# Attention and feed-forward on one core: a guard flag computed under held-back value products, and input loads in tiles

## The reference

```python
xn = layernorm(x)
q, k, v = xn @ Wq.T, xn @ Wk.T, xn @ Wv.T          # q: 4 groups x 8 heads x 16, k and v: 8 heads x 16
probs = softmax(q k^T * 16**-0.5)                  # per batch, group and head, over 2048 keys
a_dot = probs @ v
sigma_q = elu(q.reshape(b, s, 4, 128))
a_mem = sigma_q @ memory / (sigma_q @ memory_norm)
x = x + a_dot * (1 - w) + a_mem * w                # w = sigmoid(memory_weight)
y = float8(layernorm(x) / input_scale)             # rounded to float8_e4m3, clipped at 448
out = x + (y * input_scale) @ (weight * weight_scale).T
```

## Time and profile before

| | us |
|---|---|
| median of 3 runs | 2056.89 (2056.71 to 2058.98) |
| profiled execution | 2056.68 |
| its span | 2055.0 |
| busy: PE / ACT / DVE / POOL | 2029.6 / 1934.2 / 1112.6 / 83.8 |
| first projection on the chain | 16.41 |
| chunk 7's first projection | 182.07 |
| first exponential | 211.51 |

### The profile page before, as it was taken

The page is one execution under the profiler, slowest core; times in us unless marked ns, Lnnn a source line. Parts: engine busy times, 40 slices in busy tenths (PEclk is TensorE's granted clock), DMA queues, the critical chain, the costliest instruction groups (busy, mean ns, idle before and its releaser), DMA issues.

```text
span 2055.0 us, 63328 instructions
## 1 busy us (share of the span) xinstructions
PE 2029.6 (99%) x27756; PEld 905.6 (44%) x27756; DVE 1112.6 (54%) x1721; ACT 1934.2 (94%) x2181; POOL 83.8 (4%) x141
## 2 busy tenths in 40 slices
PE   8999999999999999999999999999999999999998
PEld 4555344434444444444444444444444444444445
DVE  5776544555455554555545555455554555545555
ACT  4555899999999999999999999999999999999997
POOL 3322000000000000000000000000000000000000
PEclk9999999999999999999999999999999999999999
DMA  5656211112211211112211222111112111121111
GB/s 193 195 187 207 63 47 29 43 49 51 51 33 48 72 51 45 34 47 70 51 47 38 69 51 51 48 48 50 50 51 50 54 49 51 51 64 35 47 49 46
DMA packets 137563, 131.64 MB, mean 64 GB/s; under 512 B 31520, under 2 KB 113824, under 8 KB 137312
## 3 DMA queue, kind: packets, MB, share of 16 engines
q1 hardware_dynamic: 135248, 125.11, 22.0%
q10 hardware_dynamic: 2064, 2.69, 0.4%
HBM read 86.57 MB, written 37.49 MB: 60 GB/s over the span
## 4 chain that ended last, share of the span: by engine, by line
PE 97%; DVE 1%; ACT 0%; DMA 0%; issue 0%; ACTq 0%; POOL 0%; DVEq 0%; POOLq 0%
PE ps L763 43%; PE ps L785 42%; PE ps L708 6%; PE ps L823 1%; PE ps L809 1%; PE ps L723 1%; PE ps L677 1%; PE ps L876 1%; PE ps L893 1%; DMA mem_aug<-in_memory_norm 0%; PE ps L924 0%; DVE ps L1068 0%; DVE pool L956 0%; DVE parts L981 0%; PE ps L692 0%
## 5 line engine op out<-in xcount | busy, mean ns | idle before, releaser
L645 ACT ACTIVATE pool<-ps 128x1024 f32<-128x1024 f32 x1953 | 1795.2, 1158 | 9.6 <-PE ps L763 6.5
L763 PE MATMUL ps<-q_st,k_st 99*32 99x512 bf16 x16128 | 1103.8, 379 | 3.2 <-issue 3.2
L785 PE MATMUL ps<-pool,v_st 128*32 128x512 f32 (+1 forms) x8568 | 1063.1, 567 | 0.0
L763 PEld LDWEIGHTS ps<-q_st,k_st 99*32 99x32 bf16 x16128 | 451.5, 96 | 804.8 <-issue 490.3
L785 PEld LDWEIGHTS ps<-pool,v_st 128*32 128x32 f32 x8568 | 276.6, 110 | 202.9 <-issue 0.5
L1152 DVE STREAM_TRANSPOSE by_token<-ps 128x512 f32<-128x512 f32 x63 | 45.2, 717 | 476.7 <-PE ps L785 476.7
L1145 DVE SCALAR_TENSOR_TENSOR parts<-parts 128x1024 f32<-128x1024 f32 x189 | 231.6, 1225 | 6.5
L1131 DVE TENSOR_SCALAR parts<-ps 128x512 f32<-128x512 f32 x126 | 87.1, 691 | 131.6 <-PE ps L763 131.6
L708 PE MATMUL ps<-pool,wqT 128*128 128x512 f32 x256 | 111.4, 593 | 0.0
L600 ACT ACTIVATE parts<-ps 128x512 bf16<-128x512 f32 x40 | 23.9, 597 | 62.6 <-PE ps L708 62.6
L1208 DVE SCALAR_TENSOR_TENSOR y_out<-ps,scalars,resid 128x512 f32 (+1 forms) x28 | 21.0, 751 | 112.9 <-PE ps L809 112.9
(11 more groups left out here) (126 smaller groups left out, 836.8 us busy)
## 6 DMA issues: line engine op xcount, KB each, us to landing
q_st<-q_aug SPq DMA_DIRECT2D x384, 64.0 KB
v_st<-v_aug SPq DMA_DIRECT2D x64, 256.0 KB
q_aug<-parts SPq DMA_DIRECT2D x96, 128.0 KB
k_st<-k_aug SPq DMA_DIRECT2D x64, 192.0 KB
sigma_kept<-y_out SPq DMA_DIRECT2D x32, 256.0 KB, 3.9
k_st<-k_aug SPq DMA_DIRECT2D x64, 128.0 KB
wqT<-sigma_kept SPq DMA_DIRECT2D x32, 256.0 KB, 3.4
resid<-in_x SPq DMA_DIRECT2D x7, 1024.0 KB, 8.9
```

Of the source, the lines that this page charges most:

```text
L645: act.activation(held[:, half_u * 2 * CH:half_u * 2 * CH + 2 * CH], sc[unit % SLOTS].rearrange("p a b -> p (a b)"), ACT.Exp, scale=EXP_UNIT)\
L763: last = pe.matmul(dst[VW * c:VW * c + VW, :], k_st[0:AUG, par, keys:keys + VW], q_st[0:AUG, par, q * CH:q * CH + CH], start=True, stop=True)
L785: last = pe.matmul(acc[par][VW * c:VW * c + VW, :].rearrange("v (i s) -> v i s", s=VW)[:, places, :], v_st[:, par, j, :], by_place[:, c, p ...
```

## The change

- Loads: chunk 0 of x comes as four DMAs of one tile and Wq as four of 128 rows, the first two of Wq on ScalarE's queue, the others on SP's once x's first tile has landed; Wk, Wv and the small loads move to SP's queue behind them. Statistics of chunk 0 wait for each tile.
- Start on TensorE: 20 turns of the identity come first; Wq is turned by row blocks as they land; the last two strips of x are turned between the first projection's matmuls; Wk's and Wv's turns and copies come after that projection. ScalarE loads its table at the start, with an exponential that nothing uses. The exponential of the memory weight and the wait for the scalars come later.
- The rows of ones of the key operand come by DMA instead of a GpSimd memset.
- Key norms of chunk c move behind the first projection of chunk c + 1, their reduction behind VectorE's first rest there.
- Chunk 6 has no value product. In chunk 7 the query norms come before the last matmul pair of the key projection, then the values of chunk 6 (in bank 1) and 7, with the key norms, the mean key norm and the ranges' turns between their tiles. The squares of chunk 7's keys are taken by ScalarE from PSUM. VectorE takes the guard's sums first, the key's rest after them, and the last two third parts after the flag.
- Two units of scores are computed before TensorE reads the flag; `scores_ready` is raised for them after it.
- VectorE's late tile uses `work`, decoding and rounding use `parts`. Its waits for stores move: for the parts to the decoding, for sigma behind the first chunk's heads.
- Tail: product 2 comes before turn 3, and between them 20 turns of the identity.

The core of the diff:

```diff
+            for t in range(TPC):
+                act.dma_start(resid[:, t, :], x_tiles[:, t, :]).then_inc(x_tile_loaded[t], 16)
+            for a in range(KT // 2):
+                act.dma_start(wq_raw[:, a, :], Wq[a * P:a * P + P, :]).then_inc(wq_loaded[a], 16)
...
+            sp.wait_ge(x_tile_loaded[0], 16)
+            for a in range(KT // 2, KT):
+                sp.dma_start(wq_raw[:, a, :], Wq[a * P:a * P + P, :]).then_inc(wq_loaded[a], 16)
...
-            pool_e.memset(k_st[ROWS:P, :, :], 1.0).then_inc(ones_set, 1)
...
+            def square_keys(c):
+                act.wait_ge(proj_ready, c * (QG + 1) + QG + 1)
+                act.wait_ge(n2_ready, 2 * c)
+                act.activation(k_sq[:, :], pj[(c * (QG + 1) + QG) % len(pj)], ACT.Square).then_inc(sq_ready, 1)
...
+            for i in range(WARM_UP_TURNS):
+                pe.transpose(n2[:, 0:P], ident[:, :], ident[:, :])
...
+                    if c > 0 and o == 0:
+                        key_norms(c - 1)
...
+            def last_chunk(c, par):
+                for o in range(QG + 1):
+                    pe.wait_ge(part3_ready, c * (QG + 1) + o - len(pj) + 1)
+                    if o < QG:
+                        project(c, par, o, range(KT))
+                    if o == 0:
+                        key_norms(c - 1)
+                project(c, par, QG, range(KT - 1))
+                query_norms(c)
+                project(c, par, QG, range(KT - 1, KT))
+                project_v(c - 1, 1 - par, 0)
+                key_norms(c)
+                for t in range(1, TPC):
+                    project_v(c - 1, 1 - par, t)
+                    if t == TPC - 2:
+                        mean_key_norm(1)
+                pe.wait_ge(v_tile_ready, c - 1)
+                project_v(c, par, 0)
+                pe.wait_ge(range_ready, 2)
...
+                last.then_inc(ranges_ready, 1)
+                for t in range(1, TPC):
+                    project_v(c, par, t)
...
-            pe.wait_ge(w_copied, 2)
-            turn_xn(0, range(KT))
-            pe.wait_ge(w_copied, KT + 2)
-            pe.wait_ge(scal, 4)
...
+            turn_xn(0, range(KT // 2))
+            pe.wait_ge(w_copied, KT)
+            for k in range(KT // 2):
+                project(0, 0, 0, range(k, k + 1))
+                turn_xn(0, range(KT // 2 + k, KT // 2 + k + 1))
+            project(0, 0, 0, range(KT // 2, KT))
+            for j in (KT, KT + 1):
+                turn_weight(j)
...
+            pe.wait_ge(part3_ready, NG * (QG + 1) - 2)
+            score_early_units()
 
             pe.wait_ge(wide_ready, 1)
             bound_too_wide = pe.value_load(wide[0:1, 0:1], min_val=0, max_val=1)
...
+            for u in range(EARLY_UNITS):
+                pe.wait_ge(early_scores, u + 1)
+                pe.sem_inc(scores_ready, 1)
+            pe.wait_ge(v_tile_ready, NG + ONE_FREE)
+            pe.wait_ge(part3_ready, NG * (QG + 1))
...
+            last_ffn_product(TPC - 2)
+            for i in range(WARM_UP_TURNS):
+                pe.transpose(last_ffn[TPC - 1][:, 0:P], ident[:, :], ident[:, :])
+            last_ffn_turn(TPC - 1)
...
+            def last_chunk(c):
+                for o in range(QG):
+                    add_sigma(c, o)
+                    rest(c, o)
+                    if o >= 1:
+                        last_part(c, o - 1)
+                    else:
+                        largest_norm(c - 1, 1)
+                largest_norm(c, 0)
+                largest_norm(c, 1)
+                sum_keys(c)
+                guard_sums(1)
+                guard_products(1)
+                rest(c, QG)
+                guard_range(1)
```

More of the change, by code:

```diff
@@ L127, in attention_ffn @@
         scalars = sb("scalars", [P, 10], F32)
-        mem_w, e_neg, one_plus, w_mem, w_dot, ws_col, s_col, inv_s, sw = (scalars[:, i:i + 1] for i in range(9))
+        mem_w, e_neg, one_plus, w_mem, w_dot, ws_col, s_col, inv_s, sw, spare = (scalars[:, i:i + 1] for i in range(10))
         s_raw = sb("s_raw", [P, 1], BF16)
@@ L534, in chunk @@
                         pool_e.wait_ge(bound_root, 1)
+                    if last and o == QG:
+                        continue
                     pool_e.wait_ge(part1_ready, i + 1)
@@ L703, in chunk @@
                         pe.wait_ge(part3_ready, i - len(pj) + 1)
-                    for k in range(KT):
-                        if o == 0:
-                            pe.wait_ge(xnT_ready, c * KT + k + 1 + TWO_FREE)
-                        w = wqT[:, k, o * P:o * P + P] if o < QG else wkT[:, k, :]
-                        last = pe.matmul(pj[i % len(pj)], w, xnT[:, par, k, :], start=(k == 0), stop=(k == KT - 1))
-                    last.then_inc(proj_ready, 1)
+                    if c == 0 and o == 2:
+                        pe.wait_ge(w_copied, KT + 2)
+                    if c > 0 or o > 0:
+                        project(c, par, o, range(KT))
+                    if c > 0 and o == 0:
+                        key_norms(c - 1)
                     if first_guard and o == 1:
@@ L712, in chunk @@
                         mean_key_norm(0)
-                if not last_chunk:
-                    turn_xn(c + 1, range(KT // 2))
+                turn_xn(c + 1, range(KT // 2))
                 query_norms(c)
-                pe.wait_ge(v_tile_ready, c + 1)
                 if first_guard:
                     pe.wait_ge(bound_in, 2)
-                for t in range(TPC):
-                    if last_chunk and t == TPC // 2:
-                        key_norms(c)
-                    for k in range(KT):
-                        last = pe.matmul(vp[:, t * P:t * P + P], xnT[:, par, k, t * P:t * P + P], wvT[:, k, :],
-                                         start=(k == 0), stop=(k == KT - 1))
@@ new lines, in strip, with unit_scores @@
+            def strip(dst, par, j, q):
+                for c in range(P // VW):
+                    keys = j * P + c * VW
+                    last = pe.matmul(dst[VW * c:VW * c + VW, :], k_st[0:AUG, par, keys:keys + VW],
+                                     q_st[0:AUG, par, q * CH:q * CH + CH], start=True, stop=True)
+                return last
+            def unit_scores(unit, par, j, half_u):
+                for x in range(2):
+                    last = strip(sc[unit % SLOTS][:, x, :], par, j, 2 * half_u + x)
+                return last
```

262 lines of the change are left out of this document (165 added, 97 removed).

## The result

The changed kernel takes 2049.28 us in the median of 6 runs (2047.13 to 2051.07), the kernel before 2056.80 in its 6: 7.5 us less, a ratio of 0.9961 (95% interval 0.9948 to 0.9974). That is inside the forecast range (2043.2 to 2051.0), 2.8 us above the forecast value of 2046.5, and the gain is 7.5 where 10.4 was forecast. The profiled execution took 2050.10; its span is 2047.8, 7.2 less than the span before.

A forecast was written before the change was run, and what follows sets the result against it. TensorE (busy 99%) and ScalarE (94%) were taken as the bound. Gains of 2.7 (start), 1.6 (chunk 4), 4.6 (end of projections with entry) and 1.5 (tail), 10.4 together, took 2056.68 to 2046.3, with 0.2 back 2046.5; range 2043.2 to 2051.0.

The forecast's parts named there:

- the forecast's own sign: Forecast wrong if the first exponential comes after 206.5, or if exponentials start more than 0.92 apart.
- rival A: Flag not covered: TensorE's read or the range stands behind the early units; gain 2.2 instead of 4.6, 2048.9; chance 0.14.
- Rival B: Loads slower in pieces: Wq's last at 12.6 instead of 8.6 leaves 0.3 of the start's gain, 2048.9; chance 0.14.
- Start: Up to the second projection: normalised x ready at 10.8, that projection at 17.1 instead of 19.84; gain 2.7.
- Chunk 4: Key norms' wait of 2.24 for VectorE goes, mean key norm comes 0.60 late; gain 1.6.
- End of the projections: Chunk 6 to the guard's flag: chunk 7 starts earlier, the guard's chain is covered; ScalarE starts heads 4.0 earlier.
- 0.85 lost: Chunk 7's third x strip waits for ScalarE's copy of the first; strips end at 2.95 instead of 2.1.
- Rival C: Clock stays low at the last product or at Wq's turns, x's turns and first projection; up to 2050.3; chance 0.07.
- The flag: End of chunk 7: flag ready some 2 us before the value products end; TensorE's read after the early units takes 1.6.
- Entry and tail: Clock stays up entering the head phase, gain 0.6; last product at full clock ends at 2050.2 instead of 2051.76, gain 1.5.
- rival D: VectorE's late exponentials slower in the work tile: over 1.5 times as long, every head waits; 2300 at double price; chance 0.03.

The follow-up runs named there:

- e7: Changed kernel with chunk 0 of x as one load again and Wq in four, all on ScalarE's queue; 2048.43 us.
- e1: Changed kernel with the prefetch of heads 0 and 1 split over chunks 5 and 6 instead of all in chunk 5; 2045.66 us.
- e4: Changed kernel with chunk 6 keeping its value product, so only chunk 7's is held back behind the norms; 2047.08 us.
- e3: Changed kernel with 24 turns of the identity filling TensorE's gap in chunk 6 before the third strip; 2048.21 us.
- e11: Kernel before the change, with the prefetch split over chunks 5 and 6 as in e1; 2056.90 us, ratio 0.9999.
- e5: Changed kernel with the key norms of chunks 0 to 5, and their reduction, back behind their value products; 2048.80 us.
- e12: Changed kernel with e1 and e5 together: split prefetch, key norms of chunks 0 to 5 back behind their value products; 2049.35 us.
- e9: The changed kernel once more, unaltered, in another series; 2048.02 us.
- after: The changed kernel itself, as first measured and profiled, against the kernel before; 2049.28 us, ratio 0.9961.
- e8: Changed kernel without the tail's 20 turns of the identity; product 2 still comes before turn 3; 2049.17 us.
- e6: Changed kernel without the 20 turns of the identity at the start; 2046.97 us.

## Why the forecast came out as it did

The time fell inside the range, but the working did not hold as it stands, and the forecast's own sign says so: it was to be wrong if the first exponential came after 206.5, and it came at 206.96. By the time alone rivals A and B (2048.9 each) fit 2049.28 better than the forecast does; only the traces rule them out. That the range held was partly luck: it was wide enough for a miss in the largest term that none of the rivals described.

**Start, 1.0 short.** Statistics of the last tiles waited 1.07 for their load and ended at 7.37, not 6.7, so x was ready at 11.12, not 10.8. From there to the second projection the forecast counted 6.3 and it takes 6.86, in every trace with this start. The last 0.16 is the forecast's base, the chain's 16.41 for the record's 16.25. Wq's last part, issued by SP, landed at 9.46 and not near 8.6, and ScalarE's last copy ended at 10.79, still ahead of x. Rival B was right in its direction and wrong in its size: the statistics of x's last tile began at 6.68 (5.97 to 7.13 in the ten traces with this start), while x in one load was there at 6.03 before and at 6.06 in e7. The splits still win, since the statistics of the first tile begin at 3.50. The Trainium skill, page "DMA: Bandwidth & Descriptors", section "Bandwidth", would have loads of at least 1 MiB for three quarters of the peak. The traces agree in so far as the whole of x was there sooner in one load (in nine of ten), and show that this isn't what the start needs: the normalised x was ready 1.2 us earlier with four loads of 256 KB than in e7.

**Chunk 4, 0.4 better.** The mean key norm's wait came as worked out (0.62 for 0.60), but the idle time in a row isn't all that a wait costs. From its first projection to chunk 5's, chunk 4 took 26.14 before (109.26 to 135.40) and takes 24.15 now (107.31 to 131.46), where a chunk without a wait takes 23.25. So the waits cost 2.9 and 0.9, not 2.24 and 0.60; the forecast had the 2.9 as chunk 4's extra length and priced the term by the row.

**End of the projections: the step that failed is "0.85 lost".** It priced the strips by ScalarE's two copies in chunk 0, where no store is waited for ahead of them. In chunk 6 ScalarE first has to write parts whose buffers SP's queue frees late. Before, these waits did not even arise: SP's second prefetch group started 1.6 us ahead of chunk 6. In the kernel before:

```profile
157.11 3.45 SPq L379 DMA_DIRECT2D q_st<-q_aug  x6
...
158.66 13.90 PE L708 MATMUL ps<-pool,wqT 128*128 128x512 f32 x32
```

and in the changed kernel, where SP's group starts at 156.64:

```profile
154.71 3.60 PE L762 MATMUL ps<-pool,wqT 128*128 128x512 f32 x8
```

The change itself brings TensorE there 3.95 us earlier and SP only 0.5, and by the table the store waits go with that lag: none at -3.7 and -1.6, 3.1 at 0.6, 4.4 to 6.7 from 1.4 on. That goes over few traces; the test is e1, which takes the prefetch out of the way and the waits with it. The value product of chunk 6 would still have hidden most of them from TensorE (e4), but it had moved on. From the first strip's turns to the next projection 5.64 pass; before, it was 6.07, or 2.16 without the value product and the key norms (3.91). So 3.5 is lost instead of 0.85, 2.7 too much, and 1.7 more because the clock fell behind the wait (e3). In e1, without store waits, the stretch takes 3.04: 0.88 lost, which is the forecast's own figure. The forecast named SP's queue for the late stores, where it was harmless, and not for these. Rival C was right that the clock would fall somewhere, and named the wrong places.

**The flag, 1.3 better.** Flag at 203.6, two us before the value products end: rival A is refuted. I took 1.6 for its read behind the early units; ScalarE starts 0.35 after they end. Most of the read runs beside the matmuls, which e4 shows from the other side: with the flag only 0.36 ahead of the units' end, 1.05 passed behind them.

**Entry and tail.** The clock is 1.00 at 212 us. Behind the first exponential (5.23 and 0.58 idle before it) ScalarE's idle time in the group went from 4.4 to 3.7 and its busy time from 1795.2 to 1794.8: 1.0 for 0.6. The tail came out as worked.

**Slower (rival D)** is refuted by the page's group of late steps; they take in the work tile what they took in the parts tile:

```profile
L1293 DVE SCALAR_TENSOR_TENSOR work<-work 128x1024 f32<-128x1024 f32 x189 | 231.6, 1225 | 6.5
```

The terms again: 2.7 - 1.0, 1.6 + 0.4, 4.0 - 2.7 - 1.7 + 1.3, 0.6 + 0.4, 1.5: 7.1 (7.2 by the spans, 7.5 in the medians).

## What to carry to other kernels

Before work is moved away from between two stages, look for what it hides on the other engines: list what the next waited-for engine itself waits for, down to the queue that issues the stores which free its buffers. A gain upstream is also a change of that queue's slack, so a wait that the trace of before doesn't have can appear two stages later, and the cure may be in the queue's order: moving half of the prefetch one chunk on gave 2.4 to 3.6 us here (e1, 2045.66, against the changed kernel's 2048.02 and 2049.28, each from another series; no run of e1 is as slow as the fastest of the changed kernel's eight) and nothing in the kernel before (e11). It is the version to keep: 11.8 us under the kernel before in the same series.

## What the runs showed of the hardware that I had not expected

- The clock falls behind some waits of TensorE and not behind others of the same length: after 2.25 in chunk 4 it fell in e5 and e12 and not before the change (2.24); after 2.24 and 3.12 in chunk 6 it fell (e9, after), in e8 it fell after 2.85 and cost 1.4, in e7 after 2.85 it didn't fall. Each other fall in the projections cost 1.7 us. What decides is open; it wasn't tried by itself.
- Turns of the identity, which compute nothing, raise the clock and hold it: with them a turn of Wq takes 0.13, without them 0.23 (e6); the projection behind the gap 3.60 and 5.29 (e3, after); the last product 1.04 and 1.73 (after, e8).
- The same six loads took SP's queue 2.94, 4.21 and 4.75 us to issue in the profiled executions of e6, e9 and the changed kernel, the last two of the same program. With it went smaller store waits and first exponentials 3.5 and 1.3 us before the changed kernel's in e6 and e9; why the time varies is open.
